# Attention with a head in each half of the array: score products of 64 rows, and the row maxima added by a second product

## The reference

```
qkv = einsum('bsi,oi->bso', x, W_qkv);  Q, K, V = split(qkv, 3)
Q, K = apply_rope(to_heads(Q)), apply_rope(to_heads(K))
scores = einsum('bhqd,bhkd->bhqk', Q, K) / sqrt(d_k)
scores = where(causal, scores, -inf)
attn = softmax(scores, axis=-1)
out = einsum('bhqk,bhkd->bhqd', attn, V)
```

## Time and profile before

| | us |
|---|---|
| median of 3 runs | 1719.1 (1715.95 to 1721.22) |
| the profiled execution's own time | 1713.8 |
| its span in the trace | 1712.1 |
| PE products busy in the span | 1522.8 (89%) |
| DVE busy | 1000.7 (58%) |
| ACT busy | 734.9 (43%) |

### The profile page before, as it was taken

One profiled execution on the slowest core, in us unless ns is written; L12 is line 12 of the kernel. 1 busy time (PEld: TensorE's weight loads), 2 busy tenths in 40 slices (PEclk: granted clock), 3 DMA queues, 4 the chain that ended last, 5 costly groups with the idle time before them and its releaser, 6 DMA issues. The chain is left out here.

```text
span 1712.1 us, 31150 instructions
## 1 busy us (share of the span) xinstructions
PE 1522.8 (89%) x9903; PEld 1138.2 (66%) x9903; DVE 1000.7 (58%) x3394; ACT 734.9 (43%) x1537; POOL 575.6 (34%) x1009
## 2 busy tenths in 40 slices
PE   6999999982999999588588999999999679579988
PEld 3777777762999999344365666666666468458877
DVE  3344544442332323378877888888888258645558
ACT  3444444420222222233325777776777523234420
POOL 3123333334000000478452323333222227735530
PEclk9999999985999999799889999999999979789999
DMA  7001111113777776478879767667664276755546
GB/s 224 1 25 44 47 47 47 35 50 130 223 207 218 206 216 190 148 226 293 263 115 190 99 93 116 91 92 112 94 94 69 63 227 204 188 134 156 157 154 206
DMA packets 170062, 235.21 MB, mean 137 GB/s; under 512 B 25040, under 2 KB 121936, under 8 KB 169776
## 3 DMA queue, kind: packets, MB, share of 16 engines
q1 hardware_dynamic: 134128, 171.55, 43.4%
q0 software_dynamic: 13008, 35.57, 6.3%
q10 hardware_dynamic: 22768, 26.11, 4.8%
HBM read 147.90 MB, written 84.98 MB: 136 GB/s over the span
## 5 line engine op out<-in xcount | busy, mean ns | idle before, releaser
L1983 ACT ACTIVATE t_probs<-t_ps_st 128x512 f32<-128x512 f32 x576 | 313.1, 596 | 134.9 <-PE t_ps_st L2037 125.4
L1964 DVE CUSTOM_DVE_ANT_0 t_seen<-t_ps_s,t_later 128x512 bf16<-128x512 f32 (+3 forms) x512 | 285.8, 587 | 22.9 <-PE t_ps_s L2023 20.8
L2037 PE MATMUL t_ps_st<-t_qs,t_ks 128*128 128x512 f32 (+3 forms) x768 | 244.0, 367 | 7.3 <-ACT t_probs L1983 5.7
L2023 PE MATMUL t_ps_s<-t_ks,t_qs 96*128 96x512 f32 (+3 forms) x768 | 248.7, 364 | 0.5 <-ACT t_neg_max L1976 0.5
L1936 POOL TENSOR_SCALAR_AFFINE_SELECT t_probs<-t_probs 128x128 f32<-128x128 f32 x512 | 137.3, 300 | 316.3 <-ACT t_probs L1983 314.6
L2037 PEld LDWEIGHTS t_ps_st<-t_qs,t_ks 128*128 128x128 f32 x768 | 137.5, 190 | 81.6 <-ACT t_probs L1983 43.7
L1964 DVE CUSTOM_DVE_ANT_0 t_seen<-t_ps_s,t_later,t_first_max 128x512 bf16<-128x512 f32 (+3 forms) x256 | 140.6, 549 | 50.7 <-PE t_ps_s L2023 50.7
L1524 POOL DMA_INDIRECT d_ye<-outputs_dram,r_pos_all x64 | 64.8, 1013 | 297.2 <-POOLq L1304 279.4
L2053 PE MATMUL t_ps_o<-t_probs,t_vs 128*17 128x256 f32 (+1 forms) x2560 | 155.7, 362 | 0.5 <-issue 0.5
L2023 PEld LDWEIGHTS t_ps_s<-t_ks,t_qs 96*128 96x128 f32 x768 | 139.4, 191 | 18.0 <-DVE t_first_max L1964 1.6
L1345 PE MATMUL m_ps_h<-m_xt,m_w_t 128*128 128x128 f32 x1136 | 140.2, 277 | 0.0
(11 more groups left out here) (329 smaller groups left out, 2690.6 us busy)
## 6 DMA issues: line engine op xcount, KB each, us to landing
m_w_t<-in_w_dram SPq DMA_DIRECT2D x71, 512.0 KB, 4.1
t_qs<-qkt_dram SPq DMA_DIRECT2D x124, 128.0 KB, 5.8
t_ks<-qkt_dram SPq DMA_DIRECT2D x124, 128.0 KB, 6.0
m_x_t<-gathered_dram SPq DMA_DIRECT2D x79, 128.5 KB, 2.1
m_x_t<-gathered_dram SPq DMA_DIRECT2D x71, 128.0 KB, 3.8
outputs_dram<-m_y ACTq DMA_DIRECT2D x71, 128.0 KB, 4.0
qkt_dram<-d_hi ACTq DMA_DIRECT2D x32, 256.0 KB, 4.5
qkt_dram<-d_lo SPq DMA_DIRECT2D x32, 256.0 KB, 5.6
```

The lines of the kernel that those rows point to most:

```text
L1964: nc.vector.tensor_tensor_reduce(out=seen[:, (NP * p + x) % (RS + 1), 0:keys], in0=bank_of(p, x)[:, 0:keys], in1=masks, scale=1.0, scalar= ...
L1983: nc.scalar.activation(probs[:, p % 2, i // NST, base:base + STC], ps_st[(NX * p + i) % RT][:], ACT.Exp, scale=HD ** -0.5).then_inc(exp_re ...
L2023: nc.tensor.matmul(bank_of(p, x)[:, 0:keys], q[0:MAX_ROW, head, qc * P:(qc + 1) * P], k[0:MAX_ROW, head, k0:k0 + keys], start=True, stop=T ...
L2037: last = nc.tensor.matmul(ps_st[(NX * p + i) % RT][:, col:col + width], k[:, head, kc * P:(kc + 1) * P], q[:, head, q0:q0 + width], start= ...
```

## The change

A head now has one half of the array's rows: head 0 uses partitions 0 to 63, head 1 uses 64 to 127, and the tiles `t_qs` and `t_ks` lose their dimension of heads. Their fetches are again 8 DMAs of 128 KB, each of 32 partitions ordered by channel, then part. A piece's product has 64 rows of one half. The pieces are ordered so that the two heads' pieces of one shape follow each other.

The maxima have tiles of their own: `maxima[p % 2]` holds the negated maxima of head 0 in partition 0 and of head 1 in partition 64, moved there by two DMAs, with zeros elsewhere; `first_ones` holds ones in these two partitions. A chunk's product no longer adds them. Each one is followed by a second product, `first_ones` with `maxima`, that accumulates into the same bank. So a chunk now has two products for each one of before, and `chunk(p, n)` issues chunk `n` of both heads: score product of head 0, of head 1, then the maxima's product of head 0, of head 1. A pair has 9 steps of two chunks, the lag is 14 steps, the turned maxima are again at step 2, and the pieces are 2 or 4 in a step. `t_ps_st` still has three banks and `t_ps_s` four. `take_out` stands one step after the last rounds of `average`, and one step before round 0 of the next pair.

```diff
 def load_heads(eng, p, q, k, qkt_dram, loaded):
-    for part in range(4):
-        load_head_rows(eng, p, q, 0, part, part % 2, qkt_dram, loaded)
-        load_head_rows(eng, p, k, 1, part, part // 2, qkt_dram, loaded)
+    rows = qkt_dram.rearrange("(l w n d) t -> l w n d t", l=2, w=2, d=HD)
+    cols = bass.ts(p // PAIRS, SEQ)
+    for h in range(2):
+        head = (p % PAIRS) * 2 + h
+        for part in range(2):
+            half = slice(h * KS + 2 * part * HD, h * KS + 2 * (part + 1) * HD)
+            eng.dma_start(q[half].bitcast(FP32), rows[:, 0, head, :, cols].rearrange("l d t -> d l t")).then_inc(loaded, 16)
+            eng.dma_start(k[half].bitcast(FP32), rows[part, 1, head, :, cols].unsqueeze(1).broadcast_to([HD, 2, SEQ])).then_inc(loaded, 16)
...
-    ks = [k_first] + [sb(f"t_ks{i}", [P, 2, SEQ], FP32R) for i in range(1, RINGQ)]
-    qs = [q_first] + [sb(f"t_qs{i}", [P, 2, SEQ], FP32R) for i in range(1, RINGQ)]
+    ks = [k_first] + [sb(f"t_ks{i}", [P, SEQ], FP32R) for i in range(1, RINGQ)]
+    qs = [q_first] + [sb(f"t_qs{i}", [P, SEQ], FP32R) for i in range(1, RINGQ)]
+    maxima = [sb(f"t_maxima{i}", [P, SEQ], FP32R) for i in range(2)]
+    first_ones = sb("t_first_ones", [P, P], FP32R)
...
-    units = [[u for i in range(NC) for u in ((0, NC - 1 - i), (1, i))], [u for i in range(NC) for u in ((0, i), (1, NC - 1 - i))]]
+    wides = [[NC - 1 - i for i in range(HALF)], [HALF + i for i in range(HALF)]]
...
+        for wide in each:
+            narrow = NC - 1 - wide
+            for qc, k0, keys in ((wide, 0, STC), (narrow, 0, (narrow + 1) * P), (wide, STC, (wide + 1) * P - STC)):
+                mine += [(head, qc, k0, keys) for head in range(2)]
...
-    upto = [(i + 1) * NP // NX for i in range(NX)]
-    avg_at = {1: (0, 1), 5: (2, 3), 9: (4, 5), 12: (6, 7), 16: (8, 9)}
-    LAG = 27
-    LAST = LAG + (pairs + 1) * NX
+    upto = [2 * ((i + 1) * NP // 2 // NST) for i in range(NST)]
+    avg_at = {0: (0, 1), 2: (2, 3), 4: (4, 5), 5: (6, 7), 7: (8, 9)}
+    LAG = 14
+    LAST = LAG + (pairs + 1) * NST
...
             def row(p):
...
                 sp.wait_ge(neg_ready, p + 1)
-                sp.dma_start(qs[s][MAX_ROW:MAX_ROW + 1].bitcast(FP32).rearrange("o h (c q) -> o (h c) q", c=NC),
-                             neg_max[:, p % 2, :].bitcast(FP32)).then_inc(row_loaded[s], 16)
+                for h in range(2):
+                    sp.dma_start(maxima[p % 2][h * KS:h * KS + 1].bitcast(FP32).rearrange("o (c q) -> o c q", c=NC),
+                                 neg_max[h * NC:(h + 1) * NC, p % 2, :].bitcast(FP32)).then_inc(row_loaded[p % 2], 16)
...
                 if live(q):
-                    exponentials(q, j)
-                if i == 3 and live(p - 1):
+                    exponentials(q, 2 * j)
+                    exponentials(q, 2 * j + 1)
+                if i == TURN and live(p - 1):
                     negate(p - 1)
-                if j == NX - 2 and live(q - 1):
+                if j == NST - 1 and live(q - 1):
                     take_out(q - 1)
...
-                nc.tensor.matmul(bank_of(p, x)[:, 0:keys], q[0:MAX_ROW, head, qc * P:(qc + 1) * P], k[0:MAX_ROW, head, k0:k0 + keys],
+                half = slice(head * KS, (head + 1) * KS)
+                nc.tensor.matmul(bank_of(p, x)[:, 0:keys], q[half, qc * P:(qc + 1) * P], k[half, k0:k0 + keys],
...
-            def chunk(p, i):
+            def chunk(p, n):
+                q, k = qs[p % RINGQ], ks[p % RINGQ]
+                if n == 0:
+                    pe.wait_ge(row_loaded[p % 2], 32 * (p // 2 + 1))
+                for kc, q0, col, width in chunks[n]:
+                    for head in range(2):
+                        at, half = NX * p + 2 * n + head, slice(head * KS, (head + 1) * KS)
+                        if col == 0:
+                            wait(pe, exp_ready, at - RT + 1)
+                        nc.tensor.matmul(ps_st[at % RT][:, col:col + width], k[half, kc * P:(kc + 1) * P], q[half, q0:q0 + width],
+                                         start=True, stop=False, skip_group_check=True)
+                    for head in range(2):
+                        at, half = NX * p + 2 * n + head, slice(head * KS, (head + 1) * KS)
+                        last = nc.tensor.matmul(ps_st[at % RT][:, col:col + width], first_ones[half], maxima[p % 2][half, q0:q0 + width],
+                                                start=False, stop=True, skip_group_check=True)
+                        if col + width == STC:
+                            last.then_inc(st_done, 1)
```

More of the change, by code:

```diff
@@ L1754, in attention @@
     VR = HD + 1
-    KS = 4 * HD
     STC = 4 * P
@@ L1838, in attention @@
     for p in range(pairs + 1):
-        for i in range(NX):
+        for i in range(NST):
             if i == TURN and p >= 1:
@@ L1905, in _ @@
         def _(pool):
[L1906 to L1910, removed]
             nc.gpsimd.memset(later[:], 0.0).then_inc(later_zeroed, 1)
+            nc.gpsimd.memset(first_ones[:].bitcast(FP32), 0.0).then_inc(rows_filled, 1)
+            for m in maxima:
+                nc.gpsimd.memset(m[:].bitcast(FP32), 0.0).then_inc(rows_filled, 1)
             pool.wait_ge(later_zeroed, 1)
@@ L1916, in _ @@
             pool.wait_ge(set_up, 1)
[L1917 to L1920, removed]
+            pool.wait_ge(rows_filled, 3)
+            for h in range(2):
+                nc.gpsimd.memset(first_ones[h * KS:h * KS + 1].bitcast(FP32), 1.0).then_inc(rows_filled, 1)
+                pool.wait_ge(rows_filled, 4 + h)
             nc.gpsimd.memset(vs[:], 1.0).then_inc(ones_filled, 1)
@@ L1931, in mask @@
             def mask(p):
-                for head in range(2):
-                    for kc, n, at in diagonals:
-                        pool.wait_ge(exp_ready, NX * p + NST * head + n + 1)
+                for kc, n, at in diagonals:
+                    for head in range(2):
+                        pool.wait_ge(exp_ready, NX * p + 2 * n + head + 1)
                         diag = probs[:, p % 2, head, at:at + P]
@@ L2029, in transpose_max @@
                 nc.tensor.transpose(ps_max(p), row_max[:, p % 2, :], ident[:]).then_inc(maxt_done, 1)
-            def chunk(p, i):
-                q, k, head = qs[p % RINGQ], ks[p % RINGQ], i // NST
-                if i == 0:
-                    pe.wait_ge(row_loaded[p % RINGQ], 16 * (p // RINGQ + 1))
-                wait(pe, exp_ready, NX * p + i - RT + 1)
-                for kc, q0, col, width in chunks[i % NST]:
-                    last = nc.tensor.matmul(ps_st[(NX * p + i) % RT][:, col:col + width], k[:, head, kc * P:(kc + 1) * P], q[:, head, q0:q0 + width],
-                                            start=True, stop=True)
-                last.then_inc(st_done, 1)
+            def chunk(p, n):
[9 more added lines that the diff above has]
+                                         start=True, stop=False, skip_group_check=True)
+                    for head in range(2):
+                        at, half = NX * p + 2 * n + head, slice(head * KS, (head + 1) * KS)
[3 more added lines that the diff above has]
+                            last.then_inc(st_done, 1)
             def average(p, r):
@@ L2045, in average @@
                 steps = [lane[r] for lane in lanes]
[L2046 to L2047 removed]
+                pe.wait_ge(exp_ready, NX * p + max(2 * place[kc, q0 // STC][0] + head + 1 for head, kc, q0, *_ in steps))
+                masks = [2 * mask_at[kc] + head + 1 for head, kc, q0, *_ in steps if q0 == kc * P]
                 if masks:
@@ L2703, in build @@
                       (moe0_loaded, 16 * (H0 // P + 2)), lambda dve, i: settle(dve, nc, kept, i))
-            q_first, k_first = (ahead.enter_context(nc.sbuf_tensor(n, [P, 2, SEQ], FP32R, side="right")) for n in ("t_qs0", "t_ks0"))
+            q_first, k_first = (ahead.enter_context(nc.sbuf_tensor(n, [P, SEQ], FP32R, side="right")) for n in ("t_qs0", "t_ks0"))
             phase(project_qkv, c, x1_dram, outputs[0], kept, x2_dram, w_qkv, rope, qkt_dram, v_dram,
```

47 lines of the change are left out of this document (18 added, 29 removed).

## The result

The changed kernel takes 1781.9 us (median of 4, 1773.5 to 1783.0) against 1720.2 us for before in the same session: 1.035 times, with a 95% interval of 1.031 to 1.039. In a later session it was 1769.5 us against 1713.5, 1.031 (1.027 to 1.036). It is slower, as forecast, but by 56 to 62 us where the forecast's terms add up to 38 (1713.8 to 1752 us). Both times lie in the range for 8 in 10 (1692 to 1790 us); the first is above the forecast's own range of 1737 to 1770, the second at its upper end.

The account below looks back on a forecast made before the run. PE was taken to bound the kernel at 14.49 us a pair. Profiled 1713.8 us + 34.5 (1.15 a pair over 30 periods) + 4 at the stage's end gave 1752 us; own range 1737 to 1770, 8 in 10 from 1692 to 1790.

Parts of the forecast that it names:

- Side by side: On PE, two heads' products in separate row halves run together, loads included: pieces' columns fall from 4.4 to 2.2 us a pair.
- PE's columns do not decide: PE's work falls to 12.3 us a pair, but new waits cost 3.3 against 2.2 gained: +1.15 a pair.
- relief-pays rival: Waits overlap, so less PE work pays and DVE bounds: 13.2 us a pair, 1675 us in all; chance 0.24.
- the point given against it: The first exponential's chain behind a chunk, 0.77 + 0.60 us, is longer than PE's 0.8 in a step without average.
- the chain: From chunk to exponential to freed bank: a step's second head waits for the previous step's first exponential, 0.77 + 0.60 us.
- The walk through one period: One pair followed step by step through PE, ACT and the banks: 15.65 us against 14.49.
- The two waits: PE's chunks wait for exponentials without average, 0.5 us each; the fourth piece behind the transpose waits for `negate`, 1.0 us later.
- The term that was mis-sized: DVE has 12.1 us to do in 15.65; its delay at four-piece steps is 0 to 0.3 a pair, taken as 0.
- The transpose among 64-row products: On PE, the maxima's transpose changes tiling mode and drains the engine: some 0.13 us more, 4 over the stage, left out.
- Start and end: The stage's end, chunks and averages without pieces, goes from 17 to 21 us, +4; memsets at the start taken as 0.
- The sum again: Total time: 1713.8 profiled, + 34.5 for 30 periods of the stage, + 4 for its end, 1752 us.
- The DMAs: Fetches stay hidden, 0; the maxima's DMA lands at 13.05 us of the period, before the 13.6 of step 0.

Follow-up runs that it names:

- e2: The changed kernel without the second product of each chunk, so the negated maxima are not added to the scores: 1735.3 us, 1.007 times before.
- e1: The changed kernel with the transpose of the maxima ahead of its step's chunk on PE, and negate ahead of that step's exponentials on ACT: 1760.4 us.
- e3: The changed kernel with DVE reducing only the first half of each piece's keys, without the causal mask there: 1765.9 us, 1.025 times before.
- e7: The changed kernel with transpose and negate ahead of their step's chunk and exponentials, and all pairs taking wide blocks from the last down: 1766.8 us.
- e10: The changed kernel unaltered, measured again in a later session: 1769.5 us, 1.031 times before.
- e6: The changed kernel with each chunk's products ordered score 0, maxima 0, score 1, maxima 1: 1766.4 us, 1.028 times before.

## Why the prediction was right, and where it was short

**Side by side.** Right, in products and in loads: 0.23 us for two.

**PE's columns do not decide.** Right. The forecast had PE fall to 12.3 us of work a pair and lose 3.3 to waits. Measured: 15.96. The relief-pays rival (13.2) failed at the point given against it; e2 shows that the chain stays long even with 2.2 us of columns less.

**The walk through one period.** Right, and closer than the mean tells. The short periods follow it to 0.13 us (15.52 against 15.65). What the forecast lacks is the long one.

**The two waits.** Both are in the rows: chunks for exponentials in steps without average (1.42 forecast and measured), the fourth piece for t_neg_max in each pair. The second was priced too high: the forecast's step has it 1.0 late, and taking the wait away gives 0.65 in a short period, 0.16 in a long one, where DVE stands right behind it (e1).

**The term that was mis-sized.** "two four-piece steps meet it within 0.2 us of its end, worth 0 to 0.3 a pair; I take 0." It is 0.3 to 0.4 in the mean (e3: 15.96 to 15.6), all of it in the downward pairs. The two loads' waits for DVE in a long period, 0.27 and 0.36 us, stand at one such step and right behind the other, and give 0.32 a pair in the mean. I had worked out DVE's total, 12.1, and not what each step asks of it, in which order. The 2.6 us in the step of the transpose add their own wait only once the wait for t_neg_max is gone (e7). The value taken should have been the upper end.

**The transpose among 64-row products.** I left out 0.13 us for it. The rows show that it costs something: its record begins 0.22 behind the last products and the next piece's 0.20 behind it, where before the follower came 0.03 later. That agrees with the Trainium skill (TensorEngine Tiling, Key Properties), by which a change of tiling mode drains the engine. With it and DVE's 0.3 to 0.4, the 15.65 becomes 16.1, a little more than measured. No run took the transpose away, so its price a pair is not shown.

**Start and end.** The end was forecast at +4; from the last transpose to the last average it was 19.7 us and is 23.9, +4.2. The start was taken as unchanged and is not: the first transpose comes 886.6 - 869.4 = 17.2 us after the first piece, where it took 13.6. There the filler products of the full array alternate with pieces of 64 rows, and each change of form leaves the loads idle:

```profile
869.43 0.18 PEld L2022 LDWEIGHTS t_ps_s<-t_ks,t_qs 64*128 64x128 f32 x2 [0.33 <-issue]
869.86 0.73 PEld L2067 LDWEIGHTS t_ps_st<-causal,ident 128*128 128x128 f32 x4 [0.24 <-issue]
```

The start is 3.6 us longer. That the changes of form are the cause is argued from these rows, no run took the fillers away; with DVE's work halved (e3) it still took 16.3 us.

**The sum again.** Against the profiles, e10 to before: stage 500.2 - 456.0 = 44 where the forecast had 34.5; start 4; end 4; behind the attention 5. That is 57 of the 57.6 us between the two spans (1769.7 - 1712.1). The first profile of the changed kernel has 46 for the stage and 14 behind the attention.

**The DMAs.** The fetches are hidden, as said. The maxima's DMA is not always: PE's loads waited for it 20 times over the stage, 10.8 us in all, 0.3 a pair. The forecast had it land 0.5 us early.

## What to carry to other kernels

Halving the work of the busiest engine can be worth nothing, as here, if the same edit turns a fine-grained hand-over into a pairwise one: count the banks in units of what one step takes, and follow one period through the waits before counting columns. An entry of another kind in a ring of banks, such as the maxima here, sets the time at which the entry one ring length behind it can go, so look at what stands there after a reorder. For an engine with 15% to spare, add up its work in each step and in the order of the pieces, not only in the period. And where a packed form needs a second pass for lack of one row, see whether a row can be freed.

## What the runs showed of the hardware that I had not expected

The fetches of Q and K got lighter. Size and count are the same, but each now fills 32 partitions, in the order channel, then part, where it filled 16 with two heads beside each other. They land after 2.9 us where it was 5.8 and 6.0, and the share of the DMA engines' time fell from 0.69 to 0.27 in the steady part. Which of the two, the number of partitions or the order, does it, no run tells. Their issue on SP takes longer:

```profile
L1742 SPq DMA_DIRECT2D t_qs<-qkt_dram x124: 552/592/1139, 861.8 to 1349.6; - x124
```

```profile
t_qs<-qkt_dram SPq DMA_DIRECT2D x124, 128.0 KB, 2.9
```

Median 592 ns, against 423 before. Neither is on the path here. The two halves of the rows work side by side for fp32r: loads and products of the two heads begin within some 0.01 us of each other, and both at the full rate. And they do not keep the program's order between them. In e6 the score product of head 1 starts with that of head 0, ahead of the product of head 0's maxima that the program has before it.
